# One VectorE reduction over four PSUM banks in place of two over two banks each

## The chip, the cores and the metric

The kernel runs on one core of a Trainium2 chip. The metric is the device time of one execution in microseconds, as the median of several runs. The core's engines work in parallel, each through its own queue in order, and meet only at semaphores: TensorE (PE) multiplies and transposes into PSUM, VectorE (DVE) and ScalarE (ACT) read PSUM and write SBUF, GpSimd (POOL) works on SBUF, SyncE (SP) issues most DMAs. PSUM has eight banks of 512 fp32 per partition.

## The reference

One block of a hybrid network on x of shape (4, 256, 32, 32), in four parts:

```python
x = _L0_conv_ref(x, ...)                     # attention over the 1024 pixels, 128 channels, 1x1 convolutions
t = _to_tokens(x)                            # (4, 1024, 256)
t = t + _L1_attn_ref(_ln_t(t), ...)          # the second attention: 8 heads of 32
t = t + _L1_ffn_ref(_ln_t(t), ...)           # 8 experts, the best 2 of each token

# inside _L1_attn_ref
dots = jnp.einsum('bhid,bhjd->bhij', q, k) * scale
attn = jax.nn.softmax(dots, axis=-1)
out = jnp.einsum('bhij,bhjd->bhid', attn, v)
out = out.transpose(0, 2, 1, 3).reshape(b, n, dim)
return out @ w_out + b_out
```

The softmax needs the maximum over 1024 keys of each query and head: 4 batches x 8 heads x 1024 queries.

## The kernel before

The program has three stages: the first attention (to about 290 us), the second attention (to about 740 us, with the tail of each batch woven into the next one), and the experts with the closing scatter (to the end).

The second attention goes through 4 batches of 32 steps, `t` in a batch and `n` in all. A batch has 8 units, 4 heads by 256 queries each; a unit has 4 steps, each with two blocks of 128 keys. In a step TensorE makes four chunks of scores (`score_chunk`, L1335), transposed, keys on partitions; ScalarE takes their exponentials (L953); two steps later TensorE weighs the values with them (`weigh_heads`, L1307) and sums them over the keys (`sum_heads`). For the sums GpSimd first adds the two key blocks (L699, summed at L1322), or, in the steps that `direct` names, TensorE sums both (L1317).

The maxima are made ahead, in a pass of their own, 7 steps earlier. In each step TensorE makes one group (`max_group`, L1254): 128 queries of 4 heads against 512 keys, each head into one PSUM bank, heads 0 and 1 into `PP[2]`, heads 2 and 3 into `PP[3]`. VectorE takes the maxima over the 512 keys (`reduce_heads`, L1741) into `mxp`. After four groups a unit is complete: VectorE joins the halves (`join_halves`, L1747), TensorE transposes the 8 columns into a row (`max_row`, L1263), VectorE copies it out (`keep_row`, L1755), and SyncE's queue stores it as the 97th row of the queries (`store_max`), so that the score product subtracts the maximum itself. This happens at t = 1, 5, 9, ..., 29: a row step. SyncE's queue has the loads of the next batch behind these stores.

The small products of TensorE that aren't part of a group share two half banks in `PP[2]` (`slot_bank`): the row of maxima, in batches 1 to 3 also eight projections of the finished batch (`tail_project`, t = 2, 3, 4, 6, 7, 8, 10, 11; L1023, 128x264), the ranks at t = 17, in the last batch a count at t = 20. They take turns by `next_slot`.

TensorE's order in a step: chunks 0 to 2, the group of maxima, chunk 3, weighing, sums, then the small product if the step has one. VectorE's: what is left of the unit before, part 0 of the tail, the maxima of heads 0 and 1, part 1 of the tail, the maxima of heads 2 and 3, part 2, the copy of the row, the projection's addition. The parts are small steps of the router (L1793 to L1920), placed by tables such as `PICK_AT`; from part to part each waits for the one before (`last_kept`). The order on all queues is written out by hand.

Two waits of TensorE hang on the maxima. The semaphore `mx_kept` stands at 2n when groups 0 to n - 1 of the count are reduced, since each of a group's two reductions adds 1. The lines are:

```python
# max_group, before group n
pe.wait_ge(s("mx_kept"), b * (2 * STEPS) + 2 * n)
# next_slot, before a small product; group[0] is the last group made
pe.wait_ge(s("mx_kept"), b * (2 * STEPS) + (2 * group[0] + 1))
```

Both also wait for `c_kept`, which counts the small products that VectorE has copied out.

Of the kernel before, what the change touches and what calls it, by code (L numbers as in the profile page):

```python
# [5 lines left out]
F32 = mybir.dt.float32  # L6
F16 = mybir.dt.float16
I32 = mybir.dt.int32
ALU = mybir.AluOpType
ACT = mybir.ActivationFunctionType  # L10
X_AXIS = mybir.AxisListType.X

P = 128
# [3 lines left out]
HALF = 512  # L17
IC = 128
HEADS, D = 8, 32
GH = 4  # L20
# [72 lines left out]
def group_place(n):  # L93
    unit, i, k = n // 4, n // 2 % 2, n % 2
    return unit // 4 % 2, unit % 4 * QN + i * P, k
# [19 lines left out]
def hybrid_block(nc, x, wk, bk, wv, bv, wq, bq, wwg, bn1_g, bn1_b, bn1_m, bn1_v, wout, bout,  # L115
                 bn2_g, bn2_b, bn2_m, bn2_v, w_qkv, w_out, b_out, wr, w1, b1, w2, b2, out):
    ctx = ExitStack()

    def sem(name):
        return ctx.enter_context(nc.semaphore(name))  # L120
# [15 lines left out]
    with ctx:  # L136
        def sb(name, shape, dt):
            return ctx.enter_context(nc.sbuf_tensor(name, shape, dt))

        WB = sb("WB", [P, E, WE], F16)  # L140
        WORK = sb("WORK", [P, 17664], F32)
        PP = [ctx.enter_context(nc.psum_tensor(f"PP{i}", [P, 2 * HALF], F32)) for i in range(4)]


        identf = sb("identf", [P, P], F32)
# [19 lines left out]
        mxp = sb("mxp", [P, 2, 2, GH, 2], F32)  # L165
# [149 lines left out]

        SCORES = [PP[0][:, 0:HALF], PP[0][:, HALF:2 * HALF], PP[1][:, 0:HALF]]
        WEIGHED = PP[1][:, HALF:2 * HALF]

        def early_bank(j):
            return PP[2 if j < 8 else 1]  # L320

# [3 lines left out]
        def qk_bank(u, last):  # L325
            return PP[(2, 3, 2, 0)[u]] if last else PP[(u + 2) % 4]

        TURNED = ((PP[1], (6, 7)), (PP[3], (3, 4, 5)), (PP[2], (0, 1, 2)))

# [5 lines left out]
        def slots_before(b, first):  # L335
            return FIRST_SLOTS - UNITS if first else b * BATCH_SLOTS + (FIRST_SLOTS - BATCH_SLOTS)
# [3 lines left out]
        def slot_bank(before, k):  # L340
            odd = before % 2 if isinstance(before, int) else FIRST_SLOTS % 2
            return PP[2][:, (odd + k) % 2 * HALF:((odd + k) % 2 + 1) * HALF]

# [11 lines left out]
        def s(name):  # L355
            if name not in S:
                S[name] = sem(name)
            return S[name]
# [1156 lines left out]
        def _(dve):  # L1515
# [218 lines left out]
                dve.wait_ge(s("c_made"), before + (at + 1))  # L1734
                return slot_bank(before, at)

            def reduce_heads(n, b, h):
                _, _, k = group_place(n)
                i = n // 2 % 2
                dve.wait_ge(s("mx_made"), b * STEPS + n + 1 - MAX_EARLY)  # L1740
                dve.tensor_reduce(mxp[:, n // 4 % 2, i, h:h + 2, k], PP[2 + h // 2][:, :].rearrange("p (h n) -> p h n", h=2),  # L1741
                                  X_AXIS, ALU.max).then_inc(s("mx_kept"), 1)

            def join_halves(u, b):

# [43 lines left out]
            def tail_aggregate():  # L1789

                last_kept()
                for t in range(NT):
                    keeps(dve.bn_aggr(mv[:, t], bst[:, t]))  # L1793

            def tail_variance():

                last_kept()
                keeps(dve.tensor_scalar(small[:, 1], mv[:, :, 1], EPS, None, ALU.add))

            def tail_guess():  # L1800

                last_kept()
                dve.tensor_scalar(small[:, 5].bitcast(I32), small[:, 1].bitcast(I32), 1, None, ALU.logical_shift_right)\
                   .then_inc(s("stat1_kept"), 1)
# [8 lines left out]
            def tail_pick(part, n, before):  # L1813

                last_kept()
                weight = per_expert(w8[:, :], NT)
                if part == 0:
                    dve.wait_ge(s("c_kept"), before + slots[0])
                    keeps(dve.tensor_reduce(rs[:, 0], logit, X_AXIS, ALU.max))
                elif part == 1:  # L1820
                    keeps(dve.tensor_tensor(val, logit, per_tile(rs[:, 0]), ALU.is_equal))
                elif part in (2, 8):
                    keeps(dve.tensor_tensor(val, val, weight, ALU.mult))
                elif part in (3, 9):
                    keeps(dve.tensor_reduce(rs[:, 3], val, X_AXIS, ALU.max))
                elif part == 4:
                    keeps(dve.tensor_tensor(oh1, weight, per_tile(rs[:, 3]), ALU.is_equal))
                elif part == 5:
                    keeps(dve.scalar_tensor_tensor(out=rest, in0=oh1, scalar=-BIG, in1=logit, op0=ALU.mult, op1=ALU.add))
                elif part == 6:  # L1830
                    keeps(dve.tensor_reduce(rs[:, 1], rest, X_AXIS, ALU.max))
                elif part == 7:
                    keeps(dve.tensor_tensor(val, rest, per_tile(rs[:, 1]), ALU.is_equal))
                    keeps(dve.tensor_tensor(rs[:, 2], rs[:, 1], rs[:, 0], ALU.subtract))
                elif part == 10:
                    keeps(dve.tensor_tensor(oh2, weight, per_tile(rs[:, 3]), ALU.is_equal))
                else:
                    keeps(dve.tensor_tensor(pick16[:, :, :], oh1, oh2, ALU.add))
                    dve.wait_ge(s("rstd_kept"), n)
                    last_kept()  # L1840
                    dve.tensor_tensor(rs[:, 2], rs[:, 2], small[:, 3], ALU.mult).then_inc(s("pick_kept"), 1)
# [27 lines left out]
            def tail_gates(part, tail, n):  # L1869

                here = slice(tail * NT, (tail + 1) * NT)
                last_kept()
                if part == 0:
                    dve.wait_ge(s("gexp_kept"), n)
                    keeps(dve.tensor_scalar(rs[:, 3], rs[:, 2], 1.0, None, ALU.add))
                elif part == 1:
                    keeps(dve.reciprocal(rs[:, 4], rs[:, 3]))
                else:
                    keeps(dve.tensor_copy(meta[:, here, 0, 2].bitcast(F32), rs[:, 4]))
                    last_kept()  # L1880
                    dve.tensor_tensor(meta[:, here, 1, 2].bitcast(F32), rs[:, 4], rs[:, 2], ALU.mult)\
                       .then_inc(s("gate_kept"), 1)
# [57 lines left out]
            def attend(b):  # L1940
                first, last = b == 0, b == B - 1
                before = slots_before(b, first)
                slots[0] = 0
                row_at = None

                def tail_part(at):

                    if at in PICK_AT:
                        tail_pick(PICK_AT.index(at), b, before)
                    if at == AGGREGATE_AT:  # L1950
                        tail_aggregate()
                    if at == (AGGREGATE_AT[0], 1):
                        tail_variance()
                    if at == (AGGREGATE_AT[0], 2):
                        tail_guess()
                    if at in PLACE_AT:
                        tail_places(PLACE_AT.index(at), before, b)
                    if at in GATE_AT:
                        tail_gates(GATE_AT.index(at), b - 1, b)
                    if last and at in EARLY_AT:  # L1960
                        early_table(EARLY_AT.index(at), before)

                for t in range(STEPS):
                    n = b * STEPS + t
                    groups = max_groups(t, first, last)
                    if row_at is not None:
                        row_kept(before, row_at)
                        row_at = None
                    joined = t + LEAD - 1
                    if joined % 4 == 3 and joined >= MAX_EARLY and t and max_groups(t - 1, first, last):  # L1970
                        join_halves(joined // 4, b)
                    if not first:
                        if t in STATS_AT:
                            tail_statistics(STATS_AT.index(t))
                        tail_part((t, 0))
                    for m in groups:
                        reduce_heads(m, b, 0)
                    if not first:
                        tail_part((t, 1))
                    for m in groups:  # L1980
                        reduce_heads(m, b, 2)
                    if not first:
                        tail_part((t, 2))
                    u = row_unit(t, first, last)
                    if u is not None:
                        keep_row(b, u, before)
                        row_at = slots[0]
                    if t % 4 == 3 and 7 <= n < B * STEPS - 1:
                        invert_sums((n - 7) // 4)
                    if first:  # L1990
                        continue
                    if t in PROJECT_AT:
                        tail_project(PROJECT_AT.index(t), before, b)
# [307 lines left out]
```

## Time and profile before

| | |
|---|---|
| median of 3 runs | 1181.38 us (1180.64 to 1184.5) |
| the profiled execution | 1179.94 us, span 1177.8 us |
| mean granted clock of TensorE | 0.981 |
| PE busy | 1095.2 us, 93% of the span |
| DVE busy | 817.8 us, 69% |
| ACT busy | 629.4 us, 53% |
| POOL busy | 602.2 us, 51% |
| L1741, maxima of the second attention | 242 instructions, 287.0 us |

Busy shares are averages over stages with different limits. The second attention is about a third of the span, and within it the steps differ: with or without a small product, with or without a part of the tail. So a step is read from the timeline, from the start of one group's matmuls (L1254) to the start of the next. A line of the timeline gives the start, the duration, the engine, the source line, the operation, what it writes and reads, the count of instructions merged into it, and in brackets the idle time before it with what ended it.

### The profile page before, as it was taken

Reading aid. Unit: us, or ns where it says so; the run is one execution under the profiler, and the core shown is the slowest. Engines: PE = TensorE matmul, PEld = TensorE weight load, DVE = VectorE, ACT = ScalarE, POOL = GpSimd, SP = SyncE. Lnnn points to the kernel's source line nnn. Section 1 sums busy time; section 2 is a strip of 40 time slices with the busy share of each in tenths; the row PEclk is TensorE's granted clock in tenths of the full one; section 3 lists DMA queues with packets and bytes.
Section 4 is the critical chain, followed back from the end, with each engine's and each line's share of the span. In section 5 each row is a group of like instructions: output and inputs, shape, how many; then the busy total and the mean of one; then the engine's idle time right before and its main releaser. Section 6 shows DMA issues by size and latency. Waiting matters only on the chain.

```text
span 1177.8 us, 34627 instructions
## 1 busy us (share of the span) xinstructions
PE 1095.2 (93%) x13416; PEld 742.7 (63%) x13416; DVE 817.8 (69%) x1493; ACT 629.4 (53%) x1144; POOL 602.2 (51%) x513
## 2 busy tenths in 40 slices
PE   7999999978899999999999989899999999999995
PEld 4464645434455555555555545688989989999883
DVE  4666666666688888788878882768655656655773
ACT  3566575546577657766776665453333333333332
POOL 3425241314788763776486546167645544543540
PEclk9999999999799999999999999999999999999998
DMA  5255842625223231434153213823333323322328
GB/s 174 90 176 209 320 163 79 198 72 186 58 62 84 88 83 31 103 96 107 53 130 96 57 48 97 309 38 78 57 50 56 46 47 55 51 44 44 47 38 290
DMA packets 98908, 121.00 MB, mean 103 GB/s; under 512 B 29024, under 2 KB 76064, under 8 KB 98112
## 3 DMA queue, kind: packets, MB, share of 16 engines
q1 hardware_dynamic: 75280, 70.40, 20.0%
q0 software_dynamic: 20400, 42.08, 15.4%
q10 hardware_dynamic: 3072, 6.30, 1.5%
q8 instruction: 113, 1.85, 0.7%
q14 instruction: 43, 0.35, 0.1%
HBM read 73.10 MB, written 45.47 MB: 101 GB/s over the span
## 4 chain that ended last, share of the span: by engine, by line
PE 66%; DVE 15%; DMA 6%; issue 6%; DVEq 2%; ACT 2%; POOL 1%; SPq 1%; POOLq 0%; ACTq 0%
PE PP L1023 21%; PE PP L1450 11%; PE PP L1335 7%; DVE mxp L1741 7%; PE PP L1307 6%; PE PP L1194 4%; PE PP L1122 3%; PE PP L1254 3%; PE PP L1039 3%; DMA res_d<-WORK,lb 2%; PE PP L1317 2%; PE PP L1322 2%; PE PP L1154 1%; DVE WORK L2019 1%; DMA WORK<-v_d 1%
## 5 line engine op out<-in xcount | busy, mean ns | idle before, releaser
L953 ACT ACTIVATE WB<-PP 128x512 f32<-128x512 f32 x512 | 268.8, 604 | 143.2 <-PE PP L1335 143.2
L1741 DVE TENSOR_REDUCE mxp<-PP 128x2 f32<-128x1024 f32 x242 | 287.0, 1219 | 63.3 <-PE PP L1254 62.7
L993 ACT ACTIVATE WORK<-PP,b1c 128x256 f32<-128x256 f32 (+1 forms) x320 | 139.6, 450 | 236.6 <-PE PP L1023 198.3
L699 POOL TENSOR_TENSOR WB<-WB 128x1024 f32<-128x1024 f32 x84 | 198.6, 2365 | 87.0 <-PE PP L1322 58.0
L782 POOL DMA_INDIRECT res_d<-WORK,lb x70 | 117.9, 1684 | 154.4 <-DVE WORK L2036 141.3
L1450 PE MATMUL PP<-WB,WORK 128*128 x1704 | 193.1, 273 | 0.0
L1023 PE MATMUL PP<-WORK,WB 128*128 128x256 f16 (+1 forms) x1552 | 175.8, 273 | 2.4 <-DVE WORK L2005 1.7
L1450 PEld LDWEIGHTS PP<-WB,WORK 128*128 128x128 f16 x1704 | 164.6, 98 | 19.6 <-issue 0.2
L1023 PE MATMUL PP<-WORK 128*128 128x128 f16 (+6 forms) x1086 | 161.2, 300 | 10.6 <-DVE WORK L1658 3.6
L1335 PE MATMUL PP<-WORK 97*32 97x256 f16 x4096 | 163.1, 279 | 7.2 <-ACT WB L953 4.3
L1023 PEld LDWEIGHTS PP<-WORK,WB 128*128 (+1 forms) x1552 | 152.5, 102 | 21.6 <-issue 4.5
L666 POOL TENSOR_TENSOR WB<-WORK,WB 128x1024 f16<-128x1024 f32 x32 | 68.9, 2152 | 167.5 <-ACT WORK L841 167.4
L1023 PEld LDWEIGHTS PP<-WORK 128*128 128x128 f16 (+1 forms) x1086 | 100.4, 118 | 72.4 <-issue 21.5
L1307 PE MATMUL PP<-WB,WORK 128*32 128x256 f32 x2048 | 137.4, 388 | 2.6 <-ACT WB L939 1.4
L1335 PEld LDWEIGHTS PP<-WORK 97*32 97x32 f16 x4096 | 94.4, 97 | 71.6 <-ACT WB L953 36.4
L2019 DVE TENSOR_TENSOR WORK<-WORK 128x512 f16<-128x512 f32 (+1 forms) x160 | 101.6, 635 | 13.0 <-issue 1.3
L742 POOL DMA_INDIRECT list_d<-meta,idx x64 | 62.8, 981 | 58.4 <-PE PP L1322 15.5
L772 POOL DMA_INDIRECT WORK<-rows_d,lb x70 | 72.0, 1028 | 38.0 <-issue 34.3
L2030 DVE SCALAR_TENSOR_TENSOR WORK<-PP,WORK 128x512 f32<-128x512 f32 (+1 forms) x40 | 25.3, 631 | 94.9 <-PE PP L1450 77.9
L1307 PEld LDWEIGHTS PP<-WB,WORK 128*32 128x32 f32 x2048 | 61.5, 111 | 34.1 <-issue 11.7
L2017 DVE CAST WORK<-WORK 128x512 f16<-128x512 f32 (+1 forms) x160 | 65.8, 411 | 20.8 <-ACT WORK L993 16.5
L1254 PE MATMUL PP<-WB 32*128 32x512 f16 x484 | 48.5, 389 | 15.2 <-DVE mxp L1741 8.9
(319 smaller groups left out, 1199.8 us busy)
## 6 DMA issues: line engine op xcount, KB each, us to landing
WORK<-in_L_ffn_W_dram POOLq DMA_DIRECT2D x32, 512.0 KB, 4.0
res_d<-WORK SPq DMA_DIRECT2D x8, 1024.0 KB, 4.6
late_d<-WB POOLq DMA_DIRECT2D x1, 6144.0 KB, 19.3
WB<-late_d ACTq DMA_DIRECT2D x3, 2048.0 KB, 14.1
v_d<-WORK SPq DMA_DIRECT2D x4, 1024.0 KB, 5.6
WORK<-q_hi_d SPq DMA_DIRECT2D x16, 256.0 KB, 3.7
WORK<-v_d SPq DMA_DIRECT2D x8, 512.0 KB, 6.2
WORK<-k_hi_d SPq DMA_DIRECT2D x16, 256.0 KB, 3.8
```

The costliest lines, as they stand in the source:

```text
L699: pool.tensor_tensor(PS[n % 2], PR[n % 3][:, 0], PR[n % 3][:, 1], ALU.add).then_inc(s("pair_kept"), 1)
L772: pool.indirect_dma_start(xs[t % 2][:, a].rearrange("p s c -> p (s c)"), None, rows_d[0:(B if t >= EARLY else B - 1) * N, :], bass.Indirec ...
L782: pool.indirect_dma_start(res1_d[:, :], bass.IndirectOffsetOnAxis(ap=lb[:, t % LISTS, a, 1:2], axis=0), ysb[u][:, a], None, compute_op=ALU ...
L953: act.activation(PR[n % 3][:, c // 2, c % 2 * 2:c % 2 * 2 + 2], SCORES[m % 3] .rearrange("p (h n) -> p h n", h=2), ACT.Exp).then_inc(s("e_ ...
L993: act.activation(hid[:, k, 0:width], hidden_bank(k)[:, 0:width], ACT.Gelu, bias=b1c[:, bass.ds(e, 1), k], scale=1.0 / WSCALE)\
L1023: mm = pe.matmul(dst, lhsT, rhs, start=(n == 0), stop=(n == len(pairs) - 1))
L1254: mm = pe.matmul(PP[2 + h // 2][:, h % 2 * HALF:(h % 2 + 1) * HALF], QM[rows_at, g, at:at + P], KM[rows_at, g, k * HALF:(k + 1) * HALF], s ...
L1307: pe.matmul(WEIGHED[h * D:(h + 1) * D, 0:QN], VV[par][:, 2 * s4 + i, h * D:(h + 1) * D], PR[n % 3][:, i, h], start=(s4 + i == 0), stop=(s4 ...
L1335: mm = pe.matmul(SCORES[m % 3][r * D:(r + 1) * D, i * QN:(i + 1) * QN], KP[g][0:QK_ROWS + 1, h, keys], QP[0:QK_ROWS + 1, g, h, q:q + QN], ...
L1450: mm = pe.matmul(PP[2][:, u * HALF + a * C:u * HALF + (a + 1) * C], lhsT, rhs, start=(n == 0), stop=(n == len(pairs) - 1))
L1741: dve.tensor_reduce(mxp[:, n // 4 % 2, i, h:h + 2, k], PP[2 + h // 2][:, :].rearrange("p (h n) -> p h n", h=2), X_AXIS, ALU.max).then_inc( ...
L2019: dve.tensor_tensor(hs[u][:, 1, k, 0:width], hid[:, k, 0:width], hs[u][:, 0, k, 0:width], ALU.subtract).then_inc(s("hs_kept"), 1)
```

## The change

One instruction takes the maxima of all four heads of a group. For that `PP[2]` and `PP[3]` become two halves of one PSUM tensor of four banks, `HIGH`; the semaphore is raised by 2 when the instruction is done; part 1 of the tail moves behind the maxima. TensorE's waits stay as they are.

```diff
-        PP = [ctx.enter_context(nc.psum_tensor(f"PP{i}", [P, 2 * HALF], F32)) for i in range(4)]
+        LOW = [ctx.enter_context(nc.psum_tensor(f"PP{i}", [P, 2 * HALF], F32)) for i in range(2)]
+        HIGH = ctx.enter_context(nc.psum_tensor("HIGH", [P, 4 * HALF], F32))
+        PP = LOW + [HIGH[:, 0:2 * HALF], HIGH[:, 2 * HALF:4 * HALF]]
+        MAXIMA = HIGH[:, :]
...
-            def reduce_heads(n, b, h):
+            def reduce_heads(n, b):
                 _, _, k = group_place(n)
                 i = n // 2 % 2
                 dve.wait_ge(s("mx_made"), b * STEPS + n + 1 - MAX_EARLY)
-                dve.tensor_reduce(mxp[:, n // 4 % 2, i, h:h + 2, k], PP[2 + h // 2][:, :].rearrange("p (h n) -> p h n", h=2),
-                                  X_AXIS, ALU.max).then_inc(s("mx_kept"), 1)
+                dve.tensor_reduce(mxp[:, n // 4 % 2, i, :, k], MAXIMA.rearrange("p (h n) -> p h n", h=GH),
+                                  X_AXIS, ALU.max).then_inc(s("mx_kept"), 2)
...
                     for m in groups:
-                        reduce_heads(m, b, 0)
+                        reduce_heads(m, b)
                     if not first:
                         tail_part((t, 1))
-                    for m in groups:
-                        reduce_heads(m, b, 2)
-                    if not first:
                         tail_part((t, 2))
```

VectorE's queue in the projection steps of a later batch, before. L1741 are the maxima, L1781 and L1782 the projection's addition and the router's logits, L1787 statistics, L1747 and L1755 the join and the copy of a row:

```order
L1741 TENSOR_REDUCE mxp<-PP 128x2 x2
L1781 TENSOR_TENSOR WORK<-PP,WORK 128x256
L1782 TENSOR_TENSOR rt<-PP,lg 128x8
L1747 TENSOR_REDUCE mx<-mxp 128x8
L1787 BN_STATS bst<-WORK 128x6
L1741 TENSOR_REDUCE mxp<-PP 128x2 x2
L1755 TENSOR_SCALAR nmr<-PP 8x128
```

The same place in the changed kernel, whose lines are numbered three higher here:

```order
L1744 TENSOR_REDUCE mxp<-HIGH 128x4
L1784 TENSOR_TENSOR WORK<-HIGH,WORK 128x256
L1785 TENSOR_TENSOR rt<-HIGH,lg 128x8
L1750 TENSOR_REDUCE mx<-mxp 128x8
L1790 BN_STATS bst<-WORK 128x6
L1744 TENSOR_REDUCE mxp<-HIGH 128x4
L1758 TENSOR_SCALAR nmr<-HIGH 8x128
```

Here nothing moved, two rows became one. TensorE's queue in two such steps, which is the same before and after but for names: L1257 is the group, L1338 the chunks, L1310 weighing, L1325 sums, L1026 the projection, L1266 the row's transpose.

```order
L1257 MATMUL HIGH<-WB 128x512 x4
L1338 MATMUL PP<-WORK 32x256 x8
L1310 MATMUL PP<-WB,WORK 32x256 x8
L1325 MATMUL PP<-WB,onesf 32x256 x4
L1026 MATMUL HIGH<-WORK 128x264 x2
L1338 MATMUL PP<-WORK 32x256 x24
L1257 MATMUL HIGH<-WB 128x512 x4
```

The second place is VectorE's queue at t = 19 and 20, where the places in the lists are made whole numbers (L1867) and the gates are made (L1875 to L1881). Before:

```order
L1867 CAST idx<-rs 128x16
L1741 TENSOR_REDUCE mxp<-PP 128x2
L1875 TENSOR_SCALAR rs<-rs 128x8
L1741 TENSOR_REDUCE mxp<-PP 128x2
L1877 RECIPROCAL rs<-rs 128x8
L1924 RECIPROCAL rcp<-rcp 128x8
L1879 COPY meta<-rs 128x8
L1881 TENSOR_TENSOR meta<-rs 128x8
L1741 TENSOR_REDUCE mxp<-PP 128x2 x2
```

And after:

```order
L1870 CAST idx<-rs 128x16
L1744 TENSOR_REDUCE mxp<-HIGH 128x4
L1878 TENSOR_SCALAR rs<-rs 128x8
L1880 RECIPROCAL rs<-rs 128x8
L1927 RECIPROCAL rcp<-rcp 128x8
L1882 COPY meta<-rs 128x8
L1884 TENSOR_TENSOR meta<-rs 128x8
L1744 TENSOR_REDUCE mxp<-HIGH 128x4
```

The small operation that stood between the two halves now stands behind the one reduction.

## Rows read from the trace of the kernel before

**Rows 1.** Busy time by stretch: us, then PE, PEld, DVE, ACT, POOL, granted clock, DMA.
```profile
311.50:370.50 59.00, 56.34 (x1214) 32.49 (x1207) 49.68 (x57) 44.12 (x87) 50.37 (x25) 1.00 0.28 71
392.00:436.00 44.00, 43.37 (x766) 23.94 (x759) 35.89 (x55) 26.26 (x51) 30.45 (x16) 1.00 0.28 78
...
464.00:468.40 4.40, 4.30 (x62) 2.23 (x63) 3.04 (x8) 1.60 (x4) 0.03 (x1) 0.61 0.24 57
```

**Rows 2.** Chain of waits, first batch: start us, duration us, what.
```profile
353.47 2.37 DVE mxp L1741 x2
355.84 0.05 issue
355.88 0.42 PE PP L1254 x4
```

**Rows 3.** Chain of waits, projection steps of the second batch.
```profile
419.54 1.09 PE PP L1023 x4
420.63 0.77 PE PP L1335 x24
```

**Rows 4.** Instructions by line and shape, whole span: busy us, mean ns, idle before.
```profile
L1741 DVE TENSOR_REDUCE mxp<-PP 128x2 f32<-128x1024 f32 x242 | 287.0, 1219 | 63.3 <-PE PP L1254 62.7
...
L1705 DVE TENSOR_TENSOR WORK<-WORK 128x2048 f32<-128x2048 f32 x4 | 9.1, 2281 | 0.0
```

**Rows 5.** Timeline of a projection step, second batch, t = 7.
```profile
417.45 0.39 PE L1254 MATMUL PP<-WB 32*128 32x512 f16 x4
...
417.89 2.35 DVE L1741 TENSOR_REDUCE mxp<-PP 128x2 f32<-128x1024 f32 x2 [0.23 <-PE PP L1254]
...
419.47 1.16 PE L1023 MATMUL PP<-WORK 128*128 128x264 f32 x4
...
421.33 0.40 PE L1254 MATMUL PP<-WB 32*128 32x512 f16 x4
```

**Rows 6.** Timeline of the projection step behind a row step, t = 6.
```profile
413.32 0.40 PE L1254 MATMUL PP<-WB 32*128 32x512 f16 x4
...
413.77 2.36 DVE L1741 TENSOR_REDUCE mxp<-PP 128x2 f32<-128x1024 f32 x2 [0.59 <-PE PP L1254]
...
415.59 1.16 PE L1023 MATMUL PP<-WORK 128*128 128x264 f32 x4
```

**Rows 7.** Timeline of a row step, t = 5.
```profile
410.19 0.40 PE L1254 MATMUL PP<-WB 32*128 32x512 f16 x4
...
410.63 2.36 DVE L1741 TENSOR_REDUCE mxp<-PP 128x2 f32<-128x1024 f32 x2 [0.20 <-PE PP L1254]
...
412.21 0.27 PE L1263 MATMUL PP<-identf,mx 128*8 128x128 f32 x1
...
412.41 0.84 PE L1335 MATMUL PP<-WORK 97*32 97x256 f16 x24
...
412.91 0.27 DVE L1755 TENSOR_SCALAR nmr<-PP 8x128 f16<-8x128 f32 x1
```

**Rows 8.** Timeline, first batch: the groups at t = 21 and t = 25.
```profile
358.74 0.40 PE L1254 MATMUL PP<-WB 32*128 32x512 f16 x4 [0.18 <-DVE mxp L1741]
...
370.50 0.40 PE L1254 MATMUL PP<-WB 32*128 32x512 f16 x4 [0.22 <-issue]
```

**Rows 9.** Timeline, second batch: group and row at t = 13 and t = 21.
```profile
439.21 0.39 PE L1254 MATMUL PP<-WB 32*128 32x512 f16 x4
...
441.16 0.27 PE L1263 MATMUL PP<-identf,mx 128*8 128x128 f32 x1
...
468.39 0.40 PE L1254 MATMUL PP<-WB 32*128 32x512 f16 x4
...
470.78 0.27 PE L1263 MATMUL PP<-identf,mx 128*8 128x128 f32 x1
```

**Rows 10.** Timeline of VectorE, second batch, t = 19.
```profile
462.17 0.75 DVE L1875 TENSOR_SCALAR rs<-rs 128x8 f32<-128x8 f32 x1
462.83 1.21 DVE L1741 TENSOR_REDUCE mxp<-PP 128x2 f32<-128x1024 f32 x1
```

## The prediction

> **What bounds the kernel now.** I read the busy times by stretch first, then the chain of waits, then the timeline of single steps. The change touches only the second attention, about 290 to 706 us. Three things are to be seen there. In the first batch TensorE and VectorE are both nearly full: of 59.0 us TensorE is busy 56.3 and VectorE 49.7 [rows 1]. In the first part of a later batch, where the tail of the batch before is projected, TensorE is busy 43.4 of 44.0 us while VectorE has some 8 us to spare [rows 1]. And the chain of waits says which of the two ends last in a step: around 353 us two maxima of 2.37 us, 0.05 us of release, then the next group's matmuls [rows 2], so VectorE; around 420 us it runs from TensorE instruction to TensorE instruction, through the projection (L1023) and the score chunks behind it (L1335) [rows 3], so TensorE.
>
> **The part that is removed.** A group's maxima are two reductions of 128x1024 at 1219 ns [rows 4]; run back to back the pair takes 2.37 us [rows 2]. The trace shows no reduction of four banks. The nearest row of its size is the 128x2048 addition, 2281 ns [rows 4]. From above, the pair as it is bounds it: 2.37. From below: 2048 columns cost 1.06 us more than 1024 (2281 less 1219), so the part that doesn't grow is 1219 - 1062 = 0.157 us, and the pair less one whole such part is 2.21. I take 2.28, the row it is nearest to. So a step that waits for the whole group gains 0.09 us, and 121 groups at most 11 us.
>
> **The part that is added.** It is not in the diff's lines but in a count. TensorE does not only wait for the maxima before the next group (max_group asks for 2n, which is both halves). In every step with a small product (projection, row of maxima, ranks, count) next_slot waits for 2·group + 1: the first half of the group just made, since the small product goes into a bank of PP[2], which that half reads. With one instruction that adds 2 at its end, 2·group + 1 is only reached with the whole group. So the small product waits for 2.28 us of reduction in place of 1.22. Behind it on TensorE's queue stand the three score chunks of the next step, then the next group; ScalarE's exponentials wait for the chunks, VectorE for the group.
>
> What a slot costs, counted from the start T of the group's matmuls:
> - Projection after a projection: T = 417.45, reduction from 417.89, product at 419.47, next group at 421.33 [rows 5]. The first half was done at 419.11, so nothing waited. Now the product can start at 0.44 + 2.28 + 0.05 (the release of [rows 2]) = 2.77 after T, not 2.02: 0.75 later, and as TensorE ends last here [rows 3], the step is 0.75 longer. There are 5 such steps (t = 3, 4, 7, 8, 11) in each of three batches: 15 x 0.75 = 11.3.
> - Projection after a row step (t = 2, 6, 10): T = 413.32, reduction at 413.77, product at 415.59 [rows 6], 2.27 after T, against 0.45 + 2.28 + 0.05 = 2.78: 9 x 0.51 = 4.6.
> - Row steps at t = 1, 5, 9: T = 410.19, the transpose at 412.21, TensorE ready at 413.25 with the three chunks (412.41 + 0.84), VectorE's copy of the row over at 413.18 [rows 7], next group at 413.32 [rows 6]. Today copy and chunks end together. Afterwards the transpose starts 2.77 after T and TensorE needs the same 1.04 from there: 3.81 in place of 3.13, 9 x 0.68 = 6.1. The copy then ends about 0.3 before the chunks and costs nothing.
> - First batch: four steps with one row step take 370.50 - 358.74 = 11.76 us [rows 8]. Afterwards 3.81 for the row step and three steps at 0.44 + 2.28 + 0.05 = 2.77, together 12.1; the step behind a row step also waits for ScalarE's copy of the sums, which comes as late as the chunks, so I take 12.2. Seven such units: 7 x 0.45 = 3.1.
> - The other 13 row steps (t = 13, 17, 21 in three batches, 25 and 29 in two): the transpose stands 1.95 after T at t = 13 and 2.39 at t = 21 [rows 9], so the delay lies between 0.82 and 0.38. Some of it at t = 13 and 17 is given back by the shorter wait in the steps after: 0.45 each, 5.9. The row at t = 29 also lets SyncE's queue go on to the loads of the next batch, so its delay is not absorbed at the batch boundary.
>
> **What is given back.** The small pieces of the tail that stood between the two halves now stand behind the whole group, beside the next group's matmuls. The largest is L1875 at t = 19: 0.66 us from its start to the second half [rows 10]. Three of these are 2.0; the early table in the last batch and other pieces I put at 1.3; eight steps that wait for the whole group and have no slot, 8 x 0.09 = 0.7. Together 4.0. If the pieces turn out to hold up the next reduction instead (two dependent ones now stand back to back), this falls to 0; if all of them stood in the way, up to 8.
>
> Sum: 11.3 + 4.6 + 6.1 + 3.1 + 5.9 - 4.0 = 27.0 us. The profiled execution took 1179.94 us with a span of 1177.8; it becomes 1206.9. It lies 1.4 under the median of the runs, 1181.38, so 1208.4 against that. Everything after the attention (TensorE-bound) is only shifted.
>
> The bounds of the unknown: with 2.21 for the reduction 55 slots (24 projections, 30 rows, 1 count) are 0.07 earlier, -4; with 2.37, +5. The release of a waiting TensorE is 0.05 us in [rows 2] but 0.14 from the row's copy, which ends at 413.18, to the group at 413.32 [rows 6, 7]: up to +5. The give-back between 0 and 8: plus or minus 4. The 13 rows between 0.38 and 0.82: -1 to +5. The ends seldom meet; +15 to +38 is the forecast's own range, 1196 to 1219.
>
> The Trainium skill, Perfetto Trace Analysis, section "Optimizing Scalar/DVE Operations", has a rule for either side. One says that larger operations help throughput if the engine is saturated. The other says that where VectorE isn't saturated but makes bubbles on other engines, breaking instructions up lets work finish sooner; this change goes the opposite way. [Rows 1] and [rows 3] put the projection steps under the second rule, [rows 2] the plain steps of the first batch under the first. By the page's estimate of about 125 ns per instruction on PSUM, 121 groups would save 15 us; the sum above keeps to the 0.09 of the rows.
>
> **Rivals.**
> 1. Faster: VectorE ends last nearly everywhere, the slot's wait lies beside work. Then 121 x 0.09 = 11 us go, with up to 4 of the pieces: about 1168. For it speak the pairs of L1741 in the chain around 353 us [rows 2]; against it that in the same first batch every fourth step has a slot, and that in [rows 5] TensorE takes up the product at once. It decides if the product could start before 2.77 after T, that is if the slot did not wait for the group. The Trainium skill's first rule, named above, would bring this. Chance 0.08.
> 2. No change: TensorE's delay is given back at its next wait for VectorE, in the steps t = 12 to 20, which wait for VectorE anyway, and at the batch boundaries. That works for a wait whose end does not depend on the delayed work. Here the reduction starts from the group's matmuls, which stand behind the delayed chunks, and the boundary hangs on the row at t = 29. Half the sum would have to be lost: 1181, chance 0.05.
> 3. Much slower: TensorE's clock. After the long wait before 464 us the granted clock was 0.61 over 4.4 us [rows 1], which is 1.7 us of work lost. The new gaps are 0.5 to 0.8 us each, shorter than that one. If ten of the 55 brought such a stretch, 27 + 17 = 44 us: 1225. The other stretches of [rows 1] stand at 1.00. Chance 0.04.
>
> **How the numbers follow.** The forecast (slower by 27 us, 1208) has 0.83. Below 0.3%, or 3.5 us, a measurement of this kernel can't tell a change from none. Slower: 0.83 + 0.04 = 0.87; same 0.05; faster 0.08. The range leaves out rivals 1 and 2 and takes in part of rival 3: 1193 to 1222.
>
> **What would show it.** The maxima: about 121 reductions of 128x4 out, 2.2 to 2.4 us each, some 10 to 18 us less VectorE time in all. L1023 and L1263 (three lines further down after the change) wait for the reduction 24 and some 30 times, about 0.4 to 0.8 us each, and projection steps last 4.6 us in place of 3.88, row steps 3.8 in place of 3.13. A batch of 112 us grows by 7 to 9 us, the first by 3 to 5. The step at t = 19 gets shorter by some 0.7 us. I am wrong if the product still starts about 2.0 after its group, or if the chain through the projection steps no longer runs over TensorE and its wait for the maxima.

## The result: slower, ratio 1.025, and the profile after

Five runs of the changed kernel on the chip of the kernel before: 1211.97 us median (1209.31 to 1214.12) against 1181.4 us (1180.64 to 1184.5); ratio 1.0248, 95% interval [1.0228, 1.0268]. That is 30.6 us more, where 27.0 were forecast. The profiled execution has a span of 1209.9 us, 32.1 more than before; 31.6 of these lie between the first and the last group of matmuls of the second attention (290.07 to 736.78 us, before 290.21 to 705.28).

The costliest groups of instructions of the changed kernel (busy time, mean of one, idle time before it and what ended that):

```profile
L1744 DVE TENSOR_REDUCE mxp<-HIGH 128x4 f32<-128x2048 f32 x121 | 277.1, 2290 | 72.1 <-PE HIGH L1257 71.8
...
L1026 PE MATMUL HIGH<-WORK 128*128 128x264 f32 x128 | 37.5, 417 | 14.7 <-DVE mxp L1744 14.7
...
L1266 PE MATMUL HIGH<-identf,mx 128*8 128x128 f32 x31 | 8.6, 276 | 21.7 <-DVE mxp L1744 21.7
```

The reduction over four banks takes 2290 ns, 0.08 us less than the pair of [rows 2], and VectorE is busy 277.1 us with maxima in place of 287.0 [rows 4]. VectorE did get 9.9 us less work. But the small products in the bank HIGH (projection L1026, row L1266) now wait for the maxima, in all 36.4 us.

The chain of waits through the projection steps of the second batch, which before went from TensorE to TensorE [rows 3]:

```profile
405.15 2.30 DVE mxp L1744
...
407.50 1.16 PE HIGH L1026 x4
408.65 0.77 PE PP L1338 x24
409.42 0.35 PE HIGH L1257 x4
...
409.87 2.30 DVE mxp L1744
```

Each step is now one ring: the group's matmuls, its maxima, the projection, the score chunks, the next group, each behind the one before, 4.72 us (405.15 to 409.87). VectorE's share of the whole chain rose from 15% to 21%, although it has less to do.

The timeline of the step that answers to [rows 5] (t = 7), then of the row step at t = 5 [rows 7]:

```profile
427.36 0.40 PE L1257 MATMUL HIGH<-WB 32*128 32x512 f16 x4
...
427.87 2.29 DVE L1744 TENSOR_REDUCE mxp<-HIGH 128x4 f32<-128x2048 f32 x1 [0.29 <-PE HIGH L1257]
...
430.22 1.16 PE L1026 MATMUL HIGH<-WORK 128*128 128x264 f32 x4 [0.77 <-DVE mxp L1744]
...
432.08 0.40 PE L1257 MATMUL HIGH<-WB 32*128 32x512 f16 x4
```

```profile
418.80 0.39 PE L1257 MATMUL HIGH<-WB 32*128 32x512 f16 x4
...
421.66 0.27 PE L1266 MATMUL HIGH<-identf,mx 128*8 128x128 f32 x1 [0.77 <-DVE mxp L1744]
421.86 0.84 PE L1338 MATMUL PP<-WORK 97*32 97x256 f16 x24
...
422.63 0.40 PE L1257 MATMUL HIGH<-WB 32*128 32x512 f16 x4
```

Both small products start 2.86 us after their group (before 2.02), and TensorE stands idle for 0.77 us ahead of each. The projection step is 4.72 us long (3.88), the row step 3.83 (3.13).

The first batch, which should have been the change's best place, in the chain that answers to [rows 2]:

```profile
356.18 0.35 PE HIGH L1257 x4
...
356.56 0.02 DVEq L1743
...
356.63 2.30 DVE mxp L1744
358.93 0.05 issue
358.98 0.42 PE HIGH L1257 x4
...
359.43 0.02 DVEq L1743
...
359.49 2.30 DVE mxp L1744
```

A step without a small product lasts 2.86 us (356.63 to 359.49), as before. The 0.08 us that the reduction saves are spent ahead of it: a new piece of VectorE's queue, L1743, the wait for the group's matmuls, comes between matmuls and reduction, which starts 0.51 to 0.52 us after its group (358.98 to 359.49); in the kernel before that was 0.44 to 0.45 [rows 5, 6].

The stretches that answer to [rows 1], cut here at the starts of groups (five units of the first batch, the steps t = 0 to 10 of the second, the step at t = 20); the columns are those of [rows 1]:

```profile
311.18:374.52 63.34, 56.52 (x1206) 32.29 (x1206) 48.66 (x36) 43.88 (x87) 50.03 (x25) 1.00 0.27 66
397.93:445.36 47.43, 40.16 (x697) 21.66 (x694) 32.47 (x40) 24.19 (x48) 28.12 (x14) 1.00 0.22 59
478.55:481.47 2.92, 2.68 (x60) 1.56 (x61) 2.82 (x7) 1.84 (x5) 0.00 (x0) 1.00 0.03 1
```

The second row has one step less than its like in [rows 1]: the same eleven steps took 40.09 us before (392.38 to 432.47), with TensorE busy for 39.46. Now TensorE idles for 7.3 of 47.4 us, VectorE for 15; neither is full, they take turns. The third row is a gain: the step at t = 20 runs at clock 1.00 and takes 2.92 us, where it ran at 0.61 and took 4.29 before (464.10 to 468.39) [rows 1, 9]. What TensorE did ahead of it, in both kernels (its first group at t = 20, the kernel before first):

```profile
464.10 0.40 PE L1254 MATMUL PP<-WB 32*128 32x512 f16 x4 [1.80 <-DVE mxp L1741]
```

```profile
478.55 0.40 PE L1257 MATMUL HIGH<-WB 32*128 32x512 f16 x4 [1.06 <-DVE mxp L1744]
```

Behind 1.80 us of idling the clock fell, behind 1.06 us it didn't. The length of that wait alone doesn't decide it, though. At t = 20 the clock held at all nine steps behind 1.06 to 1.14 us (the changed kernel, experiments 2 and 3), but behind 1.79 to 1.83 us it fell at eight steps of twelve and held at four, all four of them in experiments 1, 4 and 5. One of these, in experiment 5, whose step then ran at clock 1.00 and took 2.86 us (474.11 to 476.97):

```profile
474.11 0.39 PE L1254 MATMUL PP<-WB 32*128 32x512 f16 x4 [1.81 <-DVE mxp L1741]
```

### The profile page after: what moved, and what is told of

It reads as the page before. It is cut to its first block, busy times and chain, and to the rows that moved or that the text cites. A ratio compares the mean times of both kernels' runs of the same rounds, so it can differ in the third digit from the quotient of the medians.

```text
span 1209.9 us, 34627 instructions
## 1 busy us (share of the span) xinstructions
PE 1097.5 (91%) x13416; PEld 742.4 (61%) x13416; DVE 811.6 (67%) x1372; ACT 629.0 (52%) x1144; POOL 600.3 (50%) x513
## 4 chain that ended last, share of the span: by engine, by line
PE 58%; DVE 21%; DMA 6%; issue 6%; ACT 3%; DVEq 2%; POOL 2%; SPq 1%; ACTq 1%; POOLq 0%
DVE mxp L1744 15%; PE PP L1026 14%; PE HIGH L1453 11%; PE HIGH L1026 6%; PE PP L1338 5%; PE HIGH L1125 3%; PE PP L1310 3%; PE HIGH L1257 2%; PE HIGH L1197 2%; DMA res_d<-WORK,lb 2%; PE PP L1042 2%; PE PP L1320 2%; PE PP L1197 2%; DMA WORK<-v_d 1%; PE HIGH L1412 1%
## 5 line engine op out<-in xcount | busy, mean ns | idle before, releaser
L956 ACT ACTIVATE WB<-PP 128x512 f32<-128x512 f32 x512 | 268.4, 606 | 172.3 <-PE PP L1338 172.2
L1744 DVE TENSOR_REDUCE mxp<-HIGH 128x4 f32<-128x2048 f32 x121 | 277.1, 2290 | 72.1 <-PE HIGH L1257 71.8
L1453 PE MATMUL HIGH<-WB,WORK 128*128 x1704 | 192.9, 273 | 0.0
L1453 PEld LDWEIGHTS HIGH<-WB,WORK 128*128 128x128 f16 x1704 | 164.7, 98 | 19.4 <-issue 0.2
L1026 PE MATMUL PP<-WORK,WB 128*128 128x256 f16 x1488 | 169.5, 274 | 2.5 <-DVE WORK L2005 2.2
L1338 PE MATMUL PP<-WORK 97*32 97x256 f16 x4096 | 160.7, 276 | 7.1 <-ACT WB L956 4.3
L1026 PEld LDWEIGHTS PP<-WORK,WB 128*128 x1488 | 145.7, 98 | 21.0 <-issue 3.3
L1310 PE MATMUL PP<-WB,WORK 128*32 128x256 f32 x2048 | 136.3, 385 | 5.5 <-ACT WB L942 5.5
L1338 PEld LDWEIGHTS PP<-WORK 97*32 97x32 f16 x4096 | 93.3, 96 | 71.8 <-ACT WB L956 41.1
L1026 PE MATMUL PP<-WORK 128*128 128x128 f16 (+2 forms) x652 | 85.9, 284 | 10.3 <-DVE WORK L1661 3.6
L1026 PE MATMUL HIGH<-WORK 128*128 128x256 f16 (+4 forms) x434 | 77.5, 325 | 15.1 <-DVE mxp L1744 14.7
L2030 DVE SCALAR_TENSOR_TENSOR WORK<-HIGH,WORK 128x512 f32<-128x512 f32 (+1 forms) x40 | 25.3, 631 | 95.1 <-PE HIGH L1453 84.0
L1310 PEld LDWEIGHTS PP<-WB,WORK 128*32 128x32 f32 x2048 | 61.5, 111 | 37.7 <-issue 15.2
L1026 PEld LDWEIGHTS HIGH<-WORK 128*128 128x128 f16 (+1 forms) x434 | 53.5, 143 | 41.7 <-DVE mxp L1744 26.5
```

Of the source, the lines that this page charges most:

```text
L956: act.activation(PR[n % 3][:, c // 2, c % 2 * 2:c % 2 * 2 + 2], SCORES[m % 3] .rearrange("p (h n) -> p h n", h=2), ACT.Exp).then_inc(s("e_ ...
L1026: mm = pe.matmul(dst, lhsT, rhs, start=(n == 0), stop=(n == len(pairs) - 1))
L1310: pe.matmul(WEIGHED[h * D:(h + 1) * D, 0:QN], VV[par][:, 2 * s4 + i, h * D:(h + 1) * D], PR[n % 3][:, i, h], start=(s4 + i == 0), stop=(s4 ...
L1338: mm = pe.matmul(SCORES[m % 3][r * D:(r + 1) * D, i * QN:(i + 1) * QN], KP[g][0:QK_ROWS + 1, h, keys], QP[0:QK_ROWS + 1, g, h, q:q + QN], ...
L1453: mm = pe.matmul(PP[2][:, u * HALF + a * C:u * HALF + (a + 1) * C], lhsT, rhs, start=(n == 0), stop=(n == len(pairs) - 1))
L1744: dve.tensor_reduce(mxp[:, n // 4 % 2, i, :, k], MAXIMA.rearrange("p (h n) -> p h n", h=GH), X_AXIS, ALU.max).then_inc(s("mx_kept"), 2)
```

## The experiments

The theory at this point: the time is the wait of the small product for the whole group's maxima, paid once per slot, and the width of the reduction matters little. Against it stood that the width itself, its later start, or the tail's pieces moved behind the group cost the time. Each kernel below was timed against the kernel before on one chip.

**1. The wait alone.** The kernel before with its two reductions; TensorE's small products wait for both halves.

```
-                pe.wait_ge(s("mx_kept"), b * (2 * STEPS) + (2 * group[0] + 1))
+                pe.wait_ge(s("mx_kept"), b * (2 * STEPS) + (2 * group[0] + 2))
```

> The kernel before, with its two reductions per group, but a small product (projection, row, ranks, count) waits for both halves of the group just made, not for the first alone. My theory (the loss is TensorE's wait for the whole group in the slot steps): the small product starts about 2.86 us after its group in place of 1.95 to 2.48, projection steps last 4.7 us, row steps 3.8; nothing of the tail is given back, since part 1 still stands between the halves, so the loss is larger than that of the changed kernel: about 38 us, some 1219 us (1212 to 1226). Rival (the loss comes from the four-bank instruction itself, its length or its start, or from the tail's new place): within 3.5 us of the kernel before, 1178 to 1185.

Measured: 1217.56 us against 1178.62, ratio 1.0336 [1.0299, 1.0373]. Its chain through two projection steps:

```profile
414.80 1.16 PE PP L1023 x4
415.95 0.77 PE PP L1335 x24
416.72 0.36 PE PP L1254 x4
...
417.10 2.37 DVE mxp L1741 x2
...
419.51 1.16 PE PP L1023 x4
```

The step is 4.71 to 4.72 us long, as in the changed kernel, with the old pair of reductions in it; row steps are 3.83. One digit in a wait brings all of the loss and more: the spans are 1215.6 and 1209.9. So the loss needs no wide reduction, and the rest of the change gives something back. What that is, the next two runs take apart.

**2. The change with a count of one.** The reduction adds 1 to mx_kept in place of 2, and all waits on it are renumbered; nothing else differs from the changed kernel.

```
-                                  X_AXIS, ALU.max).then_inc(s("mx_kept"), 2)
+                                  X_AXIS, ALU.max).then_inc(s("mx_kept"), 1)
```

> The changed kernel, but the one reduction raises its semaphore by 1 and the waits are renumbered for it. In the changed kernel, where it is raised by 2, the wait for the group's matmuls stands on VectorE's queue as an instruction of its own and the reduction starts 0.52 us after the group in place of 0.45. Theory (the step of 2 splits the wait off and costs 0.07 us in each step that waits for the whole group): reductions start 0.45 after the group again, plain steps of the first batch last 2.79 in place of 2.86, small products start 2.79 after their group; some 80 steps x 0.07 = 5.6 us less than the changed kernel, about 1206 us. Rival (the later start has another cause, or is hidden): as the changed kernel, 1210 to 1214. Against the kernel before it stays slower by 20 us or more by either, since the slots still wait for the whole group.

Measured: 1206.77 us, ratio 1.0241 [1.0217, 1.0266]. The interval overlaps the changed kernel's, so the whole time doesn't decide it; the trace does. Its chain in the first batch:

```profile
351.80 0.36 PE HIGH L1257 x4
352.18 2.30 DVE mxp L1744
...
354.53 0.42 PE HIGH L1257 x4
354.98 2.30 DVE mxp L1744
```

The queue's piece is gone, the reduction starts 0.45 us after its group again, and a step without a slot takes 2.80 us. Slots start 2.79 after their group, projection steps last 4.65, row steps 3.77. So adding 2 in place of 1 costs 0.07 us at each reduction, because the reduction's own wait then stands ahead of it as an instruction of VectorE's queue.

**3. The tail's pieces moved alone.** The kernel before, its two reductions and its old wait; the pieces that stood between the halves stand behind both.

```
-                    if not first:
-                        tail_part((t, 1))
                     for m in groups:
                         reduce_heads(m, b, 2)
                     if not first:
+                        tail_part((t, 1))
                         tail_part((t, 2))
```

> The kernel before with its two reductions and its waits, but part 1 of the tail stands behind both halves, as in the changed kernel. It shows by itself what the tail's new place gives. Theory: the step at t = 19 is 0.6 to 0.7 us shorter, the one behind it 1.3 us, because TensorE's clock no longer falls; the ranks at t = 17 come up to 0.8 later; in the last batch, where the early table follows, 2 to 4 us are gained. Together 3 to 8 us faster than the kernel before, 1173 to 1178 us. Rival (the pieces only stop the next reduction instead): within 3 us, or slower by the ranks, 1181 to 1184.

Measured: 1176.48 us, ratio 0.9976 [0.9959, 0.9993]. The medians differ by 2.1 us, the ratio stands for 2.8: less than the 3 to 8 expected and inside the rival's 3, so the whole time doesn't tell them apart. The steps do: 1.9 us less at t = 19, 3.4 less at t = 20 (its clock doesn't fall) and 2.2 less at the end of the last batch, 1.4 more elsewhere, 6.1 us less between the first and the last group. The 1.9 at t = 19 came the same in all three batches and belong to the moved pieces. The other two gains also turn up where the pieces stand at their old place (next section). By itself this part of the change cost nothing and gave a little.

**4. Both, each where it belongs.** Steps without a small product reduce four banks at once; steps with one keep two halves, and the first half raises a semaphore of its own, mx_half, for which the small product waits. Counts go by one.

```
-                pe.wait_ge(s("mx_kept"), b * (2 * STEPS) + (2 * group[0] + 1))
+                pe.wait_ge(s("mx_half"), slots_through(b, group[0] - LEAD))
...
+                        if halves:
+                            reduce_half(m, b, 0)
+                        else:
+                            reduce_heads(m, b)
```

> One reduction over four banks, raising its semaphore by 1, in the steps without a small product; two halves in the steps with one, the first half counted by a semaphore of its own on which the small product waits, with part 1 of the tail between them as in the kernel before. Theory: no slot waits longer than in the kernel before; 24 plain steps of the first batch and some 8 others get 0.07 us shorter (2.79), t = 19 and 20 as in the changed kernel, the last batch's table steps too: about 9 us faster than the kernel before, 1172 us (1168 to 1177). Rival (merging costs by itself, wherever it is done): not faster than the kernel with the part moved alone, or slower than the kernel before.

Measured: 1172.7 us, ratio 0.9952 [0.9936, 0.9968]: 5.9 us faster than the kernel before, less than the 9 expected. Slots start as in the kernel before (404.36 to 406.38 us, 2.02), steps without one last 2.79 to 2.80. But t = 19 did not get shorter, 5.00 us; the last section says why. Its trace is 5.8 us shorter between the first and the last group: 1.7 in steps without a small product, 1.6 at t = 20 (the clock held in one batch of three), 2.0 at the end of the last batch, the rest mostly in the first steps of the first batch.

**5. The wait at the projections alone.** The first experiment's wait, at the 24 projections only.

```
-                    bank = next_slot(b, before)
+                    bank = next_slot(b, before, halves=2)
```

> The kernel before, with its two reductions, but the matmuls of a projection (24 slots in all) wait for both halves of the maxima where they waited for the first; the row matmuls still start behind the first half. Theory (the delay is paid once at each slot whose first matmul waits, whatever the reduction's width): 15 projections behind a projection at 0.84 us (3.88 to 4.72), 6 behind a row step at about 0.59, 3 about 0.66, together some 20 us, less some 2 us that the stall at the step of the list of places gives back: 1195 to 1200 us beside 1179. Rival (a later projection is absorbed by the row matmuls that follow, or the cost sits in the row steps): 1179 to 1186 us. The row steps that follow no projection should read 3.13 us as before under either.

Measured: 1198.4 us against 1180.16, ratio 1.0149 [1.0119, 1.0178]: 18.2 us. A projection step and the row step behind it:

```profile
411.79 0.40 PE L1254 MATMUL PP<-WB 32*128 32x512 f16 x4
...
414.65 1.16 PE L1023 MATMUL PP<-WORK 128*128 128x264 f32 x4 [0.77 <-DVE mxp L1741]
416.51 0.40 PE L1254 MATMUL PP<-WB 32*128 32x512 f16 x4
...
418.53 0.27 PE L1263 MATMUL PP<-identf,mx 128*8 128x128 f32 x1
419.65 0.40 PE L1254 MATMUL PP<-WB 32*128 32x512 f16 x4
```

The projection step takes 4.72 us; the row step behind it 3.14, as before. In the trace 15 steps are longer by 12.5 us in all and 9 by 5.5. No step after them is shorter by more than 0.16, but for t = 20, by 2.35 over three batches: there the clock held in two of them, behind the same wait of 1.8 us as before. A delay on this ring is not absorbed.

**6 and 7** answer a question that the traces raised (below): in each batch after the first, the pairs at n = 18 are summed by TensorE and not by GpSimd, first in the kernel of experiment 4, then in the kernel before.

```
-DIRECT = (13, 14, 15, 16, 17) + tuple(range(19, 28))
+DIRECT = tuple(range(13, 28))
```

> The kernel of the fourth run (one reduction over four banks in the steps without a small product, two halves in the others), and the step with n = 18 of each batch joins those that sum both halves of a pair with TensorE in place of an addition on GpSimd. Theory (a small VectorE operation at steps 18 and 19 lasts until GpSimd's 2.4 us addition ends): without the addition that VectorE operation lasts 0.2 us as elsewhere, step 19 falls from 5.0 to 3.3 to 3.5 us, step 20 from 3.7 or more to about 3.3 with its four extra matmuls of 0.4 us together, 4 to 7 us of the whole in three batches: ratio to the kernel before 0.990 (0.988 to 0.992). Rival (the small operation is slow by itself, or by another GpSimd operation): step 19 stays at about 5 us, the extra matmuls add 1 us, ratio 0.996.

Measured: 1166.75 us, ratio 0.9887 [0.9864, 0.9911], the lowest median here. Step t = 19 takes 3.69, 3.45 and 3.44 us in the three batches, where 3.3 to 3.5 were expected, and t = 20 3.04, 3.04 and 3.39, where some 3.3 were.

> The kernel before with that one edit alone: the step with n = 18 of each batch is summed by TensorE, so that no GpSimd addition runs beside VectorE's small operations of steps 18 and 19. Theory: the cast that lasted 1.71 us there lasts 0.2, step 19 falls from 4.92 to about 3.3 to 3.5 us, TensorE's clock does not fall in step 20 and that step reads about 3.3 where it was 4.29, in all 5 to 7 us: ratio 0.994 to 0.996. Rival: step 19 stays at 4.9 us and the time is the same or 1 us longer, ratio 1.000 to 1.001.

Measured: 1168.94 us, ratio 0.9916 [0.9890, 0.9941], 11.2 us faster and so more than expected. Its steps t = 19 and 20 are 8.8 us shorter over three batches, the added sums at t = 20 included. The row steps at t = 17 are 1.3 longer in all, as another addition of GpSimd now comes there (last section), and one at t = 25 is 0.5 longer, which no run explains. Some 7 us of its span's 12.1 lie between the first and the last group; the rest lies behind the attention, where stretches of the same code took 467 to 475 us in the profiled executions of all these kernels, and is not put down to the edit. The intervals of experiments 6 and 7 overlap: that merging adds anything to the edit of n = 18 is not shown.

## Why the prediction was right, step by step

Between the first and the last group the changed kernel took 31.6 us more. By the prediction's terms, from the starts of the groups in both traces:

| Term | forecast | measured |
|---|---|---|
| 15 projections behind a projection | 11.3 | 12.6 |
| 9 projections behind a row step | 4.6 | 5.6 |
| 9 row steps, t = 1, 5, 9 | 6.1 | 6.3 |
| 7 units of the first batch | 3.1 | 6.4 |
| 13 other row steps | 5.9 | 5.6 |
| steps t = 14, 15, 18 | 0 | 1.4 |
| third batch, t = 9 and 10: a late reduction, then a lower clock | 0 | 1.5 |
| given back (t = 19, 20, last batch) | -4.0 | -7.1 |
| rest | 0 | -0.7 |

The total came nearer than its terms: six of them came out 8.7 us larger than forecast, the others 4 smaller, and that these partly cancel is luck. By batches the time grew by 5.7, 9.0, 10.3 and, up to the last group, 6.7 us; the prediction had named 3 to 5 for the first and 7 to 9 for the others.

- **The added wait.** Right, and shown by experiment 1: the count 2·group + 1, not the reduction's width, costs the time. Forecast was a start 2.77 us after the group, measured 2.86. The reduction at 2.29 (2.28 taken) and its release at 0.04 to 0.05 were right; the 0.07 of the split wait was missing. Experiment 2 takes it away and gets 2.79.
- **The gain of 0.09 per step.** Right as to the reduction (0.08), wrong as to the step: it stayed at 2.86, as the split wait used it up.
- **The first batch, the term most off.** A unit was to take 12.2 us and takes 12.67 (63.34 over five, in the stretches above). Two steps of it were counted 0.09 too short. The step behind the row step is 3.07 long and not 2.86: I had named its wait for ScalarE's copy of the sums but put it at some 0.1; the rows show it, with the transpose ahead:

```profile
339.44 0.27 PE L1266 MATMUL HIGH<-identf,mx 128*8 128x128 f32 x1 [0.84 <-DVE mxp L1744]
...
340.16 0.60 ACT L956 ACTIVATE WB<-PP 128x512 f32<-128x512 f32 x1 [1.95 <-PE PP L1338]
...
340.65 0.59 ACT L942 ACTIVATE WB<-PP 128x512 f32<-128x512 f32 x1
...
341.39 1.07 PE L1310 MATMUL PP<-WB,WORK 128*32 128x256 f32 x16 [0.18 <-ACT WB L942]
```

  The late transpose delays the score chunks, these ScalarE's exponential (L956), it the copy (L942), and the copy TensorE's next products. In experiment 2, where the plain steps fall to 2.80, this step stays at 3.07.
- **The other row steps.** Right in their sum. But at t = 17 the wait is not the only cause: experiment 3, with the old wait, is 0.44 us longer there too, and 0.29 longer at t = 18, where the moved pieces come later. And the steps behind (t = 14, 15, 18), which were to give some of it back, grew by 1.4 in all.
- **Given back.** t = 19 gave 2.05, forecast 2.0. Experiment 3 gets 1.9 there by the moved pieces alone, experiment 1 without them nothing. Not foreseen were 3.1 at t = 20: the clock held in all three batches (2.92, 2.93 and 3.82 us; the last batch has the count there, whose product waits 0.91 us for the maxima). The last batch gave 2.0, of 1.3 put at the early table and others. That these two come from the moved pieces is not shown: experiment 3 has them (3.4 and 2.2), but so has experiment 1, with the pieces at their old place (1.6 and 1.9), and experiment 5 has 2.35 at t = 20. In the last batch VectorE's L1908 (a product of two small tensors) took 1.57 us beside GpSimd's L712 in the kernel before and 0.21 in experiment 1, where no such addition ran: its case is that of the last section.
- **The rivals.** That VectorE bounds nearly everywhere falls with experiment 1: VectorE has the same work there and the time rises by 3.4%. That the delay is given back falls with experiment 5. The clock: the first steps of the first batch run at a low one in every kernel here (0.51 to 0.80 in the changed kernel); behind them it fell once, in the third batch, where the granted clock was 0.71 for one step.

```profile
562.36:568.27 5.91, 5.73 (x69) 3.08 (x66) 2.96 (x4) 2.56 (x6) 2.56 (x2) 0.71 0.51 130
```

That step takes 5.91 us where its like in the two other batches take 4.73; it came behind a wait of 1.12 us for the maxima (L1266 at 561.39), longer than the 0.77 of the two others, because the reduction began 0.86 us after its group and not 0.52. Why it did, no run shows. Such a wait doesn't always bring a lower clock: behind 1.09 us at t = 13 of experiment 1 it fell in one batch of three.

- **The rule against this change.** The Trainium skill, Perfetto Trace Analysis, section "Optimizing Scalar/DVE Operations", advises to break an instruction up where VectorE isn't saturated but makes bubbles on other engines. The trace agrees: two halves as against one whole are worth 0.77 us of TensorE at each projection that follows a projection. Its other figure, some 125 ns per instruction on PSUM, isn't borne out for this merge: 0.08 us between the pair and the one instruction.

## What to carry to other kernels

Before two instructions are merged, look for who waits for the first of them: here half a result let another engine go on, and that was worth ten times what one instruction less saves. A semaphore count that is merely renumbered (add 2 in place of 1 and 1) hides such a lost wait and can cost 0.07 us an instruction by itself. Merge where nobody waits for the part, and keep the halves where someone does: that version beat both kernels (ratio 0.9952), though little of it is the merging: 1.7 of its 5.8 us lie in the steps that it merges, and its interval overlaps that of the pieces moved alone.

## What the runs showed that I had not expected

At t = 18 and 19 of a later batch a small operation of VectorE lasts until an addition of GpSimd ends. The kernel before, VectorE and GpSimd:

```profile
458.71 2.38 POOL L699 TENSOR_TENSOR WB<-WB 128x1024 f32<-128x1024 f32 x1 [9.94 <-PE PP L1317]
459.04 0.21 DVE L1861 TENSOR_REDUCE rs<-rt 128x8 f32<-128x64 f32 x1
...
459.41 1.71 DVE L1867 CAST idx<-rs 128x16 int32<-128x16 f32 x1
...
461.72 1.18 POOL L712 TENSOR_TENSOR WORK<-WB,WORK 128x512 f16<-128x512 f32 x1
462.17 0.75 DVE L1875 TENSOR_SCALAR rs<-rs 128x8 f32<-128x8 f32 x1
```

The cast ends at 461.12, GpSimd's addition at 461.09; L1875 at 462.92, GpSimd's L712 at 462.90. A reduction beside the same addition takes its 0.21 us. In experiment 4, where the pieces stand elsewhere, it is another operation's turn:

```profile
456.49 2.45 POOL L712 TENSOR_TENSOR WB<-WB 128x1024 f32<-128x1024 f32 x1 [9.87 <-PE PP L1330]
456.62 2.40 DVE L1878 TENSOR_TENSOR rt<-rt 128x64 f32<-128x64 f32 x1
...
459.44 0.23 DVE L1887 CAST idx<-rs 128x16 int32<-128x16 f32 x1
```

Now the cast takes 0.23 us and a product of two small tensors 2.40, to 459.02, where GpSimd's addition ends at 458.94 (0.22 where no addition runs beside it). Without the addition, in experiment 7:

```profile
459.70 0.17 DVE L1867 CAST idx<-rs 128x16 int32<-128x16 f32 x1
...
461.06 0.16 DVE L1875 TENSOR_SCALAR rs<-rs 128x8 f32<-128x8 f32 x1
```

The cast takes 0.17, step t = 19 3.05 us in place of 4.92, and the clock holds at t = 20 (3.11 in place of 4.29). In turn another addition of GpSimd (L705, 453.43 to 454.16) now falls beside L1841 at t = 17, which lasts 0.55 us, to 454.18, in place of 0.17. So the stall of 1.80 us ahead of t = 20, of which the prediction counted the 0.66 of L1875 as VectorE's work, was mostly VectorE waiting for GpSimd. The Trainium skill, SBUF — State Buffer, section "Who interferes with whom", states a lock on a pair of ports shared by the two engines, held for a whole instruction: casts, tensor-scalar operations and those with two inputs in SBUF can be blocked by it, reductions never. These rows agree, in which operations are stretched and in that they end with GpSimd's.
